# TensorE turns the newly projected keys one chunk later in every step of a fused attention kernel

## What is computed

```python
q = einsum('bsd,ed->bse', x, Wq)          # 32 heads of 128
k = einsum('bsd,ed->bse', x, Wk)          # 8 key/value heads
v = einsum('bsd,ed->bse', x, Wv)
q, k = rope(rmsnorm(q, q_norm_w)), rope(rmsnorm(k, k_norm_w))
k_all = concatenate([k_cache[block_table], k])   # 512 cached keys, then 128 new ones
v_all = concatenate([v_cache[block_table], v])
probs = softmax(where(valid, q @ k_all.T * SCALE, -1e30))
attn  = (probs @ v_all).reshape(bsz, seqlen, 4096) @ Wo.T
x = x + down(drop_half(silu(gate(attn))) * up(attn))
x = x + int4(adapter(x))
```

## Time and profile before

| | |
|---|---|
| median of 3 runs | 1373.96 us (1373.55 to 1375.35) |
| the profiled execution: its time | 1373.65 us |
| the profiled execution: its span | 1371.8 us |
| share of the chain that ended last | PE 91%, DVE 5%, ACT 2% |
| granted TensorE clock | full in all 40 slices |

### The profile page before, as it was taken

The page is one execution under the profiler, slowest core; times in us unless marked ns, Lnnn a source line. Parts: engine busy times, 40 slices in busy tenths (PEclk is TensorE's granted clock), DMA queues, the critical chain, the costliest instruction groups (busy, mean ns, idle before and its releaser), DMA issues.

```text
span 1371.8 us, 23449 instructions
## 1 busy us (share of the span) xinstructions
PE 1356.9 (99%) x8015; PEld 1183.4 (86%) x8015; DVE 1203.7 (88%) x2624; ACT 871.3 (64%) x2224; POOL 784.2 (57%) x813
## 2 busy tenths in 40 slices
PE   9899999999999999999999999999999999999998
PEld 6788888888888888888888888888888888888888
DVE  8999898989898989898989898989899987987783
ACT  7777676767676767676767676767777662222221
POOL 7876666666667666766676667666766510111111
PEclk9999999999999999999999999999999999999999
DMA  6111211121112111111111111112121321111212
GB/s 220 45 51 43 58 55 47 43 58 53 49 41 59 54 48 43 58 55 47 43 59 55 47 43 59 54 48 74 45 71 32 110 96 45 47 47 49 76 42 75
DMA packets 34050, 80.46 MB, mean 59 GB/s; under 512 B 10274, under 2 KB 11554, under 8 KB 32514
## 3 DMA queue, kind: packets, MB, share of 16 engines
q1 hardware_dynamic: 17538, 45.29, 10.3%
q0 software_dynamic: 16384, 33.59, 8.0%
HBM read 76.74 MB, written 2.10 MB: 57 GB/s over the span
## 4 chain that ended last, share of the span: by engine, by line
PE 91%; DVE 5%; ACT 2%; issue 1%; POOL 0%; DVEq 0%; ACTq 0%
PE proj_ps L111 10%; PE proj_ps L113 10%; PE proj_ps L112 10%; PE turn_ps L772 10%; PE score_ps L113 5%; PE score_ps L112 5%; PE score_ps L111 5%; PE value_ps L111 5%; PE value_ps L112 5%; PE value_ps L113 5%; PE gu_ps L111 3%; PE gu_ps L113 3%; PE gu_ps L112 3%; PE out_ps L1037 2%; PE turn_ps L734 2%; PE turn_ps L741 2%
## 5 line engine op out<-in xcount | busy, mean ns | idle before, releaser
L1288 ACT ACTIVATE probs<-probs,shift,rstd 128x640 f32<-128x640 f32 x256 | 234.4, 918 | 120.2 <-DVE shift L1732 119.1
L563 POOL DMA_INDIRECT kg<-kc,idx x256 | 259.8, 1015 | 83.8 <-issue 77.9
L573 POOL DMA_INDIRECT vg<-vc,idx x256 | 260.3, 1017 | 70.7 <-issue 70.6
L1768 DVE TENSOR_TENSOR pt_lo<-turn_ps,pt_hi 128x512 fp32r<-128x512 f32 x320 | 217.4, 685 | 45.4 <-ACT pt_hi L1294 44.9
L1294 ACT ACTIVATE pt_hi<-turn_ps 128x512 fp32r<-128x512 f32 x320 | 187.6, 593 | 93.6 <-PE turn_ps L772 93.0
L1743 DVE CUSTOM_DVE_ANT_0 probs<-score_ps,mask 128x640 f32<-128x640 f32 x256 | 206.8, 822 | 12.0 <-PE score_ps L113 10.2
L581 POOL TENSOR_TENSOR v_lo<-vg,v_hi 128x512 fp32r<-128x512 f32 x64 | 89.1, 1391 | 207.5 <-ACT v_hi L1259 207.4
L772 PE MATMUL turn_ps<-cst,probs 128*128 128x128 f32 x1280 | 191.5, 272 | 1.7 <-DVE probs L1761 1.0
L111 PE MATMUL proj_ps<-w_hi,xt_parts 128*128 128x512 f32 x496 | 189.1, 381 | 0.7 <-ACT qk L1244 0.7
L772 PEld LDWEIGHTS turn_ps<-cst,probs 128*128 128x128 f32 x1280 | 157.1, 140 | 28.2 <-DVE probs L1761 2.2
L113 PE MATMUL proj_ps<-w_hi,xt_parts 128*128 128x512 f32 x496 | 168.2, 339 | 0.0
(11 more groups left out here) (255 smaller groups left out, 3283.4 us busy)
## 6 DMA issues: line engine op xcount, KB each, us to landing
w_raw<-wqkv SPq DMA_DIRECT2D x28, 384.0 KB, 3.2
wo_raw<-wo SPq DMA_DIRECT2D x32, 256.0 KB, 3.1
wa_sb<-wa SPq DMA_DIRECT2D x7, 1024.0 KB, 4.8
kg<-kc,idx POOLq DMA_INDIRECT x256, 2.6
vg<-vc,idx POOLq DMA_INDIRECT x256
wg_raw<-wg SPq DMA_DIRECT2D x2, 1376.0 KB, 6.1
wu_raw<-wu SPq DMA_DIRECT2D x1, 2752.0 KB, 9.3
wd_raw<-wd SPq DMA_DIRECT2D x1, 2560.0 KB, 12.6
```

What stands on the lines that cost most here:

```text
L563: pool.indirect_dma_start(kg[:, b % 2, c, :], None, kc, bass.IndirectOffsetOnAxis(ap=idx[:, s // B % 2, b * NC + c:b * NC + c + 1], axis=0))\
L573: pool.indirect_dma_start(vg[:, b % 2, c, :], None, vc, bass.IndirectOffsetOnAxis(ap=idx[:, s // B % 2, b * NC + c:b * NC + c + 1], axis=0))\
L1288: act.activation(row, row, ACT.Exp, bias=shift[:, h:h + 1], scale=rstd[:, b % 2, h:h + 1], accum_out=sums[:, h:h + 1])\
L1768: dve.tensor_tensor(pt_lo[:, at, :], turn_ps[1 - j % 2][:, :], pt_hi[:, at, :].bitcast(F32), ALU.subtract).then_inc(p_lo_done[j], 1)
```

## The change

In `step(s)`, for every step that has them, the turning of the new keys moves behind chunk 1 of the key and value projection, so that it stands between chunks 1 and 2 instead of between the value product of block 4 and chunk 1. Nothing is added or removed. The order on all other engines stays as it was. Step 0 and the work ahead of it, and the steps from 61 on, stay as they were: 60 steps change.

```diff
                         if live(s):
                             values(s, b, 4)
+                        if live(s + 3):
+                            project_kv(s + 3, b3, g3, (1,))
                         if live(s + 2):
                             turn_new_k(s + 2)
                         if live(s + 3):
-                            project_kv(s + 3, b3, g3, (1, 2, 3))
+                            project_kv(s + 3, b3, g3, (2, 3))
                         if live(s + 1):
                             turn_probs(s + 1, b1, 0)
```

## The result

| | before | after |
|---|---|---|
| median of 20 runs each, side by side | 1374.88 us (1373.54 to 1375.74) | 1376.41 us (1375.78 to 1378.21) |
| ratio of after to before | | 1.0017, 95% interval 1.0011 to 1.0023 |
| span of the profiled execution | 1371.8 us | 1374.4 us |

The account below looks back on a forecast made before the run. TensorE, busy 99%, was taken to bound the kernel. Block +0.1, late -0.1, ordinary 0, step 2 +0.2 gave +0.2 on 1373.65, so 1373.85; the median lies 0.3 higher: forecast 1374.1 us, range 1372.3 to 1375.8 (about 0.85).

Parts of the forecast that it names:

- The gain at the place: At the turning in seven block and five late steps, nearly all of TensorE's 3.4 us loss goes.
- ceiling 3.4 us: Most the change can bring: 2.0 in seven block steps plus 1.4 in five late steps, 0.25% of the time.
- Block steps: Steps with b = 4: VectorE is the bound, gain lost at next step's cached-keys load; -0.1 to +0.9, taken +0.1.
- other bound: Block steps: VectorE follows TensorE's earlier pace after all, so the gain stays, -2.0 us.
- The sign that the prediction named: Step 21 in the profile after: cached-keys load about 0.4 late, with 0.25 or more lost there.
- The b = 5 steps: Steps with `ot_lo` ahead of the rotation on VectorE: the later turning costs nothing there.
- Late steps: Five late steps, 57 the largest: turned-probabilities load still waits for `qt_lo`; -0.3 to 0, taken -0.1.
- Ordinary steps: 33 steps with b = 1, 2, 3, 6, 7: the chain behind the later turning costs 0, keeping +1.0 us as a bound.
- dead heat: Ordinary steps: output projection's load, released behind `ot_lo`, would come at 225.18 against its place 225.17; 0.03 lateness free.
- the rival "slower": Ordinary steps: output projection's load becomes the new wait; 1377.3 us at 0.1 beyond (chance 0.06), mild form 1375.3 (0.06).
- Step 2: Its output projection is already late, so later `ot_lo` costs between 0 and +0.36 us once; taken +0.2.
- the lower bound: Step 2 costs 0: `rot_q` stands until GpSimd's `ka` ends, so its later start is free.

Follow-up runs that it names:

- x5b: Kernel before, with an unused reduction over 256 columns on VectorE directly ahead of its sum of the rotated queries in b = 5 steps: 1490.53 us, ratio 1.0016.
- first set: Four kernels: old order in b = 5 steps 1373.02 us; turning moved in block steps alone 1372.27; kernel after with GpSimd held 1373.09; kernel before with GpSimd held 1373.89.
- x5c: Kernel before, with the unused 256-column reduction on VectorE ahead of its sum in b = 5 steps, measured again in the fourth set: 1374.88 us, ratio 1.0000.
- x9: Kernel after, with a 128x32 memset on GpSimd between its last gather and its remainder of the values in b = 5 steps: 1487.87 us, ratio 0.9988.
- the first experiment: Kernel after, with the turning back ahead of chunk 1 in the b = 5 steps, all other steps as changed: 1373.02 us, ratio 0.9987.
- x5: Kernel before, with four 128x8 memsets on VectorE ahead of the rotation in b = 5 steps: 1491.57 us, ratio 1.0007.

## Why the prediction was wrong, point by point

- **The gain at the place: right.** No loss at the turning in step 20, ceiling 3.4 us.
- **Block steps: wrong.** The prediction let the gain of 2.0 be given back at the load of the cached keys of the next step and took +0.1. It measured -2.0, the "other bound". The failed step is the reading of the earlier trace rows: busy time was taken for work. Some 0.45 of the 16.80 went when the two normalisations and the gather shifted against each other (1.46 to 1.01), and VectorE then had time over. The sign that the prediction named, the load of the cached keys in step 21 about 0.4 late, is not there: the load starts with the matmul ahead of it.
- **The b = 5 steps: the step that failed.** "The steps with b = 5 have `ot_lo` ahead of the rotation ... both cost nothing." That looked only at the output projection. What stands last in that chain there is the sum, and behind it the maxima and the second half of the scores. Without the conflict the sum had room: held apart from GpSimd it ends 3.89 behind the later turning, 4.25 on the scale on which 5.2 is free. With it the sum waits for two of GpSimd's instructions, 2.41 instead of 0.69, in six of seven steps: +4.6. No term of the sum, no rival and no bound of the range held this. The two starts were 0.12 apart in the trace of before. The change made the sum 0.36 later, ScalarE's release of the subtraction stayed where it was, and the gain in the block steps, which the prediction had ruled out, put a gather directly ahead of the subtraction.
- **Late steps: right.** In step 57 the load of the turned probabilities still stands 0.12 behind `qt_lo` (1033.64, load 1033.76), and the step went from 17.60 to 17.59; only step 55 gained, 0.15. The sum was -0.2 against -0.1 forecast. The moved gate piece shows why.
- **Ordinary steps: right,** 17.11 against 17.13, with the dead heat where it was put (0.12 behind `ot_lo`), and two chunks cost 0.36 a step, so the rival "slower" had its mechanism and its price right but not its place.
- **Step 2: the lower bound was right.** The prediction took +0.2 between 0 and 0.36; it was 0.00. `rot_q` took 0.92 instead of 1.28: it started later and ended with GpSimd's table as before, which is the rule of the Trainium skill that spoke for 0 ("SBUF — State Buffer", section "Who interferes with whom"). The trace agrees. VectorE and GpSimd of the kernel after:

```profile
85.24 0.75 POOL L654 TENSOR_TENSOR ka<-acc 128x256 f32<-128x256 f32 x1
85.63 0.92 DVE L1685 TENSOR_TENSOR rot_q<-qk,qa 128x512 f32<-128x512 f32 x1
```

- **The sum.** Forecast of the parts: +0.1 - 0.1 + 0 + 0.2 = +0.2. Measured: block -2.0, b = 5 +4.6, late -0.2, ordinary and b = 0 -0.3, step 1 +0.4, step 2 0: +2.5. Two errors of -2.1 and +4.6 partly cancelled, so that the time came no further from the forecast than it did is luck.

**Left open.** What the turning costs when it moves in the b = 5 steps alone, without the later gathers, was not run. Step 1 was 0.37 longer in the kernel after and not with the turning moved in ordinary steps alone (17.12). But the openings differ between executions of the same code: the kernel with GpSimd held, which is the kernel after up to step 3, had 21.76 in step 0 and 18.28 in step 1, and the kernel after 20.78 and 17.66. So a single step 1 proves nothing. For the same reason the spans of these two can't be set against each other, only their steps behind the opening.

## What to carry to other kernels

Before an instruction is moved, list what hangs behind it on every engine, and for each link with two SBUF inputs on VectorE look what GpSimd does at that time: two starts that are 0.1 us apart are a race that a small shift can turn round, and the loser stands until the winner's instruction has ended, here even two of them. Look too at what stands ahead of each of the two on its own engine. An engine's busy share doesn't tell whether it is full of work; an instruction that is longer than its fellows of the same form (here 2.41 and 1.75 against 0.69, 1.73 against 1.30) may be one that waits. And if a wait comes from a piece of spare work ahead of a chain, move the piece, not the consumer.

## What the runs showed of the hardware

- **Whoever waits ends at a nearly fixed distance behind the other.** When the sum went first, GpSimd's subtraction ended 1.15 to 1.16 behind the end of the sum, whether it had started 0.12 behind the sum (before), 0.26 (x5b, step 5) or 0.48 (first set). When a subtraction went first, the sum ended 0.54 to 0.60 behind the end of the last one that it waited for (after, x5c, x9).
- **One instruction waits for two.** The sum took 0.69 alone, 1.75 when it waited for one of GpSimd's subtractions, and 2.41 when it waited for both. In step 21 of the kernel after GpSimd's second subtraction ran in its usual 0.47, right behind the first, though VectorE had long been waiting; in x5c, at the same pair, VectorE got in between and the second took 0.91. What decides that was not found.
- **The first in the records is not always the first at the port.** Starts of GpSimd's subtraction against the sum, in step 21: 0.12 behind with GpSimd idle ahead of it, the sum wins (before); 0.09 ahead, idle, GpSimd wins (x5c); 0.13 and 0.19 to 0.21 behind, but right on the heels of a gather or a memset, GpSimd wins (after, x9); 0.26 and 0.48 behind, on the heels of a gather too, the sum wins with 0.68 and 0.69 (step 5 of x5b, the first experiment). So the border in such cases lies between 0.21 and 0.26. The Trainium skill, same page and section, has issue order decide. That fits if an instruction that follows another on GpSimd asks for the port some 0.2 before its recorded start, or VectorE's asks after its own; no run here tells these apart.
- **Gathers take part.** Most gathers issued by GpSimd take 0.94 to 1.05. In step 20 one took 1.15 (before) and 1.74 (after) beside VectorE's normalisation of SBUF rows, and the pair of these took 1.46 before and 1.01 after. Other gathers are longer too, up to 1.97 in the kernel before, and not all of those stand beside a normalisation.
- **Two chips were 8% slower for every kernel,** 1487 and 1491 us, with a granted clock of 0.99 and more. There the steps with b = 5 take 17.11 to 17.18 as elsewhere (in all kernels but x9) and most others 17.6 to 20. ScalarE's timeline of the kernel with memsets on VectorE (x5), in step 31, shows a copy that starts late:

```profile
637.05 0.60 ACT L1294 ACTIVATE pt_hi<-turn_ps 128x512 fp32r<-128x512 f32 x1 [1.65 <-PE turn_ps L772]
```

The turning that it waits for ended at 635.91 by the same trace, 1.1 earlier. What kept ScalarE is not seen there, and no run here looked for it.
